# Splitting the first stage's result on two engines instead of one: ScalarE copies, GpSimd subtracts

## The reference

```python
Q = (X @ Wq.T + bq).reshape(B, S, H, d_head) * scale      # B=2, S=256, D=256, H=16
K = (X @ Wk.T + bk).reshape(B, S, H, d_head) * scale
V = (X @ Wv.T + bv).reshape(B, S, H, d_head)
scores = jnp.where(causal, einsum('bqhd,bkhd->bhqk', Q, K), -inf)
out = softmax(scores) @ V          # then @ Wo.T + bo
x = _layernorm(x + out)            # one [16, 128, 256] tensor
```

## Time and profile before

| | |
|---|---|
| median of three runs | 1124.04 us |
| the profiled execution | 1125.8 us, with a span of 1123.7 us |
| mean granted TensorE clock | 0.94 |
| TensorE busy | 994.0 us (88%) |
| VectorE busy | 885.0 us (79%) |
| ScalarE busy | 638.4 us (57%) |
| GpSimd busy | 538.6 us (48%) |
| DMA, mean | 95 GB/s |

### The profile page before, as it was taken

One profiled execution on the slowest core, in us unless ns is written; L12 is line 12 of the kernel. 1 busy time (PEld: TensorE's weight loads), 2 busy tenths in 40 slices (PEclk: granted clock), 3 DMA queues, 4 the chain that ended last, 5 costly groups with the idle time before them and its releaser, 6 DMA issues. The chain is left out here.

```text
span 1123.7 us, 25370 instructions
## 1 busy us (share of the span) xinstructions
PE 994.0 (88%) x8610; PEld 735.7 (65%) x8610; DVE 885.0 (79%) x2031; ACT 638.4 (57%) x1626; POOL 538.6 (48%) x983
## 2 busy tenths in 40 slices
PE   4769889973998977899999999999996999979996
PEld 3547666641565635788888888888884666546664
DVE  1458898932897966899999999999756899758885
ACT  2334555521798952555555555555443999944553
POOL 6347677873355643244444444444433465533322
PEclk8889999976899986899999999999998999989999
DMA  7989999843678530001001011111300566411111
GB/s 138 180 206 184 206 194 177 165 81 102 161 186 189 142 104 15 11 29 39 29 29 30 29 34 30 36 32 54 90 20 29 160 170 170 115 34 44 57 57 33
DMA packets 131550, 106.46 MB, mean 95 GB/s; under 512 B 16176, under 2 KB 124000, under 8 KB 131424
## 3 DMA queue, kind: packets, MB, share of 16 engines
q1 hardware_dynamic: 117952, 93.72, 35.6%
q10 hardware_dynamic: 11504, 8.98, 2.9%
q0 software_dynamic: 1968, 2.16, 1.2%
HBM read 64.97 MB, written 29.43 MB: 84 GB/s over the span
## 5 line engine op out<-in xcount | busy, mean ns | idle before, releaser
L406 DVE TENSOR_REDUCE ca_nm<-p_p 128x2 f32<-128x512 f32 x256 | 162.8, 677 | 16.0 <-PE p_p L304 14.3
L543 ACT ACTIVATE ca_pt<-p_p 128x512 f32<-128x512 f32 x256 | 142.6, 598 | 12.2 <-PE p_p L323 7.0
L304 PE MATMUL p_p<-ca_ks,ca_qs 96*128 96x256 bf16 x512 | 102.5, 285 | 18.1 <-DMA ca_ks<-k_stack 16.7
L1916 ACT ACTIVATE la_pq<-p_p,la_nm 128x128 f32<-128x128 f32 x256 | 90.3, 366 | 38.0 <-DVE la_nm L2019 38.0
L323 PE MATMUL p_p<-ca_qs,ca_ks 128*128 128x256 bf16 x512 | 101.3, 281 | 6.1 <-ACT ca_qs L535 2.4
L62 POOL TENSOR_TENSOR ca_pt<-la_lt,one 64x1024 f32<-64x1024 f32 x32 | 60.5, 1889 | 61.7 <-ACT la_lt L1895 60.5
L535 ACT ACTIVATE ca_qs<-p_p 32x1024 bf16<-32x1024 bf16 x64 | 65.1, 1017 | 40.4 <-PE p_p L313 38.9
L1900 ACT ACTIVATE la_qq<-p_p 128x512 f32<-128x512 f32 x32 | 19.1, 598 | 99.1 <-PE p_p L1732 99.1
L1070 DVE TENSOR_REDUCE sa_nm<-sa_p_s 128x4 f32<-128x512 f32 x64 | 43.6, 685 | 37.7 <-PE sa_p_s L930 37.3
L304 PEld LDWEIGHTS p_p<-ca_ks,ca_qs 96*128 96x128 bf16 x512 | 50.9, 102 | 31.5 <-DMA ca_ks<-k_stack 17.7
L1763 PE MATMUL p_p<-ca_pt,la_qq 128*128 128x128 f32 x512 | 70.9, 282 | 0.3 <-POOL ca_pt L62 0.3
(11 more groups left out here) (265 smaller groups left out, 2763.6 us busy)
## 6 DMA issues: line engine op xcount, KB each, us to landing
sa_qks<-sa_qkp SPq DMA_DIRECT2D x96, 128.0 KB, 5.3
ca_qs<-q_stack SPq DMA_DIRECT2D x32, 384.0 KB, 4.4
ca_ks<-k_stack SPq DMA_DIRECT2D x32, 384.0 KB, 5.3
ca_ct<-in_ctx_t SPq DMA_DIRECT2D x32, 128.0 KB, 5.1
ca_xr<-x_state SPq DMA_DIRECT2D x32, 128.0 KB, 2.1
x_state<-ca_xn SPq DMA_DIRECT2D x32, 128.0 KB, 2.1
k_stack<-sa_cxp SPq DMA_DIRECT2D x16, 192.0 KB, 2.8
q_stack<-sa_parts SPq DMA_DIRECT2D x16, 192.0 KB, 2.8
```

Of the source, the lines that this page charges most:

```text
L304: last = pe.matmul(p_s[n % 3][:, qc, :], QS[b % 4][0:STACK, h, 128 * qc:128 * qc + 128], KS[b % 4][0:STACK, h, :], start=True, stop=True)
L406: dve.tensor_reduce(NM[b % 2][:, h, :], p_s[n % 3][:, :, :], AX.X, ALU.max, negate=True).then_inc(max_done, 1)
L543: act.activation(PT[g][:, j, :, :], p_e[n % 2][:, :, :], ACT.Exp, scale=SCALE).then_inc(exp_done, 1)
L1916: last = act.activation(PQ[g % 2][:, j, :], p_s[g % 2][:, j, :], ACT.Exp, bias=NM[b % 2][:, 4 * g + j:4 * g + j + 1], accum_out=SM[g % 2][ ...
```

## The change

The result's split is taken off GpSimd in part. Its two copies (L62 on `sa_parts`) become ScalarE activations with `ACT.Copy`: `split_high(b - 2)` in slot 1 of step b, behind the exponentials and the high part of the context, and `split_middle(b - 2)` in slot 3, right behind the exponentials and ahead of the middle part of the context and the bias. The two subtractions stay on GpSimd but no longer stand together: `split_rest(b - 2)` is where the whole split was, `split_low(b - 2)` comes after `rstd(b - 1)` and `add_bias(b)`. The one counter `split_steps` becomes four semaphores; SyncE's stack stores wait for the last of them, `x_lo`. At the end of the stage the pairs follow each other in the same order.

```diff
@@ sync: store(b)
-                sp.wait_ge(split_steps, 4 * b + 4)
+                sp.wait_ge(x_lo, b + 1)
@@ gpsimd
-            def split(b):
-                pool.wait_ge(xn_done, b + 1)
-                wait(pool, xn_stored[b % 2], 16 * STORES * (b // 2))
-                wait(pool, split_steps, 4 * b)
-                split3(pool, XN[b % 2][:, :], parts[b % 2], rest[:, :], split_steps, 4 * b,
-                       lambda to, x: pool_copy(pool, sh, to, x))
+            def split_rest(b):
+                pool.wait_ge(x_hi, b + 1)
+                wait(pool, x_mid, b)
+                wait(pool, x_lo, b)
+                pool.tensor_tensor(rest[:, :], XN[b % 2][:, :], parts[b % 2][:, 0], ALU.subtract).then_inc(x_rest, 1)
+
+            def split_low(b):
+                pool.wait_ge(x_mid, b + 1)
+                pool.tensor_tensor(parts[b % 2][:, 2], rest[:, :], parts[b % 2][:, 1], ALU.subtract).then_inc(x_lo, 1)
@@ gpsimd: step(b)
                 if b >= 2:
-                    split(b - 2)
+                    split_rest(b - 2)
                 if later(b):
                     max_parts(b + 1, 1)
                 if b:
                     rstd(b - 1)
                     add_bias(b)
+                if b >= 2:
+                    split_low(b - 2)
                 if front(b):
                     query_key_rest(b + 3)
@@ gpsimd: after step 13, and at the end
                     pool.wait_ge(xb_done, b + 1)
+                    pool.wait_ge(x_lo, b - 1)
                     set_picks(pool, sh, picks_set)
-            split(B - 2)
+            split_rest(B - 2)
+            split_low(B - 2)
             rstd(B - 1)
-            split(B - 1)
+            split_rest(B - 1)
+            split_low(B - 1)
@@ scalar
+            def split_high(b):
+                act.wait_ge(xn_done, b + 1)
+                wait(act, xn_stored[b % 2], 16 * STORES * (b // 2))
+                act.activation(parts[b % 2][:, 0, :], XN[b % 2][:, :], ACT.Copy).then_inc(x_hi, 1)
+
+            def split_middle(b):
+                act.wait_ge(x_rest, b + 1)
+                act.activation(parts[b % 2][:, 1, :], rest[:, :], ACT.Copy).then_inc(x_mid, 1)
@@ scalar: step(b), after context_high in slot 1
+                    if g == 1 and b >= 2:
+                        split_high(b - 2)
+                    if g == 3 and b >= 2:
+                        split_middle(b - 2)
@@ scalar: at the end
             copy_out(B - 1)
+            split_high(B - 2)
+            split_middle(B - 2)
             copy_heads(B - 1)
+            split_high(B - 1)
+            split_middle(B - 1)
```

More of the change, by code:

```diff
@@ L741, in self_attention @@
         xn_done = sem("xn_done")
-        split_steps = sem("split_steps")
+        x_hi, x_rest, x_mid, x_lo = sem("x_hi"), sem("x_rest"), sem("x_mid"), sem("x_lo")
         xn_stored = [sem(f"xn_stored{u}") for u in range(2)]
```

## The result

The changed kernel takes 1134.68 us (median of five runs, 1132.82 to 1137.15) against 1124.04 us; the ratio is 1.0088 with a 95% interval of 1.0063 to 1.0112. Six more runs of it beside 29 of the kernel before, in a later comparison, gave 1.0098 (1.0067 to 1.0129). The forecast was 1128.6 us, slower, in a range up to 1135.5: the direction and the mechanism are right, the size is half of what came. Executions of one kernel spread by up to 13 us here (the kernel before: 1117.42 to 1130.7 in 29 runs), so a single trace shows where time goes, and the ratios say how much. A ratio takes in all runs of both kernels; it need not be the quotient of the two medians.

A forecast was written before the change was run, and what follows sets the result against it. GpSimd was taken to sit in the first stage's loop, with stack loads on SyncE having 0.7 us of slack or none. Terms +3.8 + 2.0 - 1.5 + 0.7 - 0.4 = +4.6 us gave 1128.6 us, range 1121.5 to 1135.5.

The forecast's parts named there:

- The late stores: On SyncE, stack stores wait for the later lower part, so the last stack load is issued at A + 7.6 us.
- A: The end of `add_bias` on GpSimd in a step, from which SyncE's stores and loads are timed.
- The three late steps: Steps 10 to 12 of the first stage: 13.53 us each instead of 12.27, +3.8 us in all.
- K: Time from A to the first scores two steps on: 13.6 us, against 10.5 before.
- third rival: Slower than forecast: TensorE waits lower the clock (2 us) and loads land slowly; +10.7 us, 1134.7 us, chance 0.15.
- the loop over two steps: First scores to A, then A to the scores two steps on: (13.45 + 13.6) / 2 = 13.5 us a step.
- The seven earlier steps: Steps before the three late ones, averaging 14.07 us: most of the delay hides there, +2.0 us (bounds 0 and 5).
- Step 13: Step without weight quantization: TensorE waits less for GpSimd's maxima, -1.5 us (bounds -1.9 and 0).
- `picks` and the end: After step 13 `split_low` precedes `picks`, +0.7 us; at the stage's end copies are faster on ScalarE, -0.4 us.
- The relief: Copies leaving GpSimd free the port shared with VectorE: L1430 took 1.04 us beside a copy, 0.69 without.
- My first rival: Faster: engines bound the steps, not the stores; -4.7 us, 1119.3 us, chance 0.15.
- ScalarE: Two copies of 0.41 us each added there: high one free, middle one ahead of the bias 0 (bounds 0 and 0.4).

The follow-up runs named there:

- Experiment 1: Changed kernel with SyncE issuing the late stack stores behind the next step's stack loads: 1118.12 us, ratio 0.9977; repeated, 1120.57 us, ratio 0.9966.
- 4: Changed kernel with the last subtraction of the split ahead of `rstd` and `add_bias` instead of behind them: 1126.89 us, ratio 1.0019.
- experiment 5: Changed kernel with GpSimd's scale of the quantized weights behind `split_rest` instead of ahead of the maxima: 1135.74 us, ratio 1.0101.
- experiments 2: Kernel before the change, with SyncE's stack loads put ahead of the late stores: 1125.55 us, ratio 1.0003.
- 8: Changed kernel with the loads first, plus two GpSimd copies into tiles nobody reads: 1125.30 us, ratio 1.0010.
- both orders: Stack loads ahead of the late stores and the scale behind the split: kernel before 1120.68 us, ratio 0.9973; changed kernel 1118.75 us, ratio 0.9956.
- experiment 7: Changed kernel with ScalarE's middle copy behind the bias instead of ahead of it: 1135.34 us, ratio 1.0092.

## Why the prediction was right in kind and short in size

**The late stores.** Right, step by step: the `q_stack` issues behind L1178 and L1195, the residual's load at A + 3.8, the last stack load starting at A + 7.6 in step 10 (208.5, with A = 200.95) and landing 6.3 us later, where 6.0 was taken. In step 11 it started only at A + 8.7, one issue before it having taken 1.76 us, and landed after 4.8: the same sum. Experiment 1 takes it away and 4 shortens it; both do what this chain says.

**The three late steps: the term that was mis-sized.** Forecast 13.53 us a step, +3.8 in all; measured 14.65, +7.1. K is not the reason: by its own loads it was 13.6 to 13.9. The step that failed is X, from the first scores to A, held at 13.45 in all three. It was 14.1 us in step 10, 16.9 in step 11 (200.24 to 217.17) and 13.9 in step 12, and the 3.5 us of step 11 make up the missing 3.3. In step 11 VectorE's lock made TensorE wait for 1.99 us, and the clock of 0.57 over the 4 us behind it cost about another 1.7 (an estimate: 4 x 0.43). The forecast had put the clock at nothing; only the third rival priced it, at 2 us.

How much of this is the change and how much one execution, a second profile of the changed kernel shows, from the run beside the repeat of experiment 1 (steps 10, 11 and 12):

```profile
190.01:204.80 14.79, 11.71 (x131) 8.54 (x129) 11.47 (x27) 8.90 (x22) 11.35 (x20) 1.00 0.80 143
204.80:217.24 12.44, 11.73 (x128) 8.58 (x129) 11.13 (x25) 6.77 (x17) 5.32 (x14) 1.00 0.95 170
217.24:231.71 14.47, 12.38 (x128) 8.61 (x129) 11.99 (x28) 8.59 (x22) 11.02 (x20) 1.00 0.64 130
```

Here the clock stayed at 1.00, X was 13.3, 13.7 and 13.6 us, and the steps took 41.70 us, 13.9 each: +4.9, near the forecast of +3.8. Where the clock holds, the loop over two steps comes out. In experiment 5 the lock was nearly gone and the three steps still averaged 14.6; there too X of step 11 was long, 15.8 us, at half clock behind the wait for the loads. What decides whether the clock falls is open: it fell behind 2.86 us there and stayed at 1.00 behind 2.84 us in this second profile.

**The seven earlier steps.** Forecast +2.0, measured +3.9 at step 10, of which 1.4 was there at step 3, so +2.5 in these steps; +3.7 in the second profile. I had also taken the second scores of step 3 (84.47) for its first (83.31); their average is 14.2 us, not 14.07, which changes nothing in the argument.

**Step 13.** Forecast -1.5 with -1.9 as its end; measured -3.4. TensorE's wait of 1.86 us for the maxima is gone. It seems to have had a price in clock too, which came back with it: the granted clock of the step went from 0.80 to 0.87, worth about 1.6 us (an estimate: 16.78 x 0.20 less 13.36 x 0.13).

**`picks` and the end.** Forecast +0.3, measured +0.9 from step 14 on.

The sum of the measured terms, +3.9 + 7.1 - 3.4 + 0.9, is the 8.5 us of the profiled executions. The medians lie 10.6 us apart, and two profiles can't say where the other 2 us are. One slip in the range: X - 0.4 and a landing of 5 give 12.8 us a step, not 12.9, which moves its lower end by 0.2 us.

**The relief.** VectorE's L1430 took 0.69 us on average in steps 3 to 12 after, against 0.90 before, where the row showed 1.04 and 0.69. The Trainium skill's rule on the shared ports ("SBUF — State Buffer", "Who interferes with whom") holds here for VectorE by L1443 and L1430, and for GpSimd by its L62 at 221.83, 0.65 us instead of 0.20 while VectorE's L1449 ran until 222.42. By itself it would have had the change faster, and with the stores out of the way the medians and ratios lie that way: 1.0003 against 0.9977 in experiments 2 and 1, back at 1.0010 in 8, and 0.9973 against 0.9956 with both orders. My first rival was this case, 4.7 us faster; what the runs show of it is 0.2% to 0.3%, 2 to 3 us, not clear of noise, and it was covered by 14 us of late stores.

**The third rival**, a lower clock with slow landing at 1134.7 us, has the number that came, and half of its reason. Its lower clock was there, in step 11 of the profiled execution; its slow landing was not, at most 6.3 us in steps 10 and 11. That the median came within 0.1 us of it is luck.

**ScalarE.** Costed at 0, and experiment 7 finds none.

## What to carry to other kernels

When a step of a chain is split over engines and a part of it moves to a later place in the order, look up who waits for its end, and what stands behind that wait on the waiting queue: here a store nobody needed soon held six loads that the next scores needed. Put loads with a near deadline ahead of stores that wait for late data. When a change adds waits of 1 to 3 us on TensorE, give the granted clock a term of its own: here the same kernel's three late steps took 43.94 us in one profile and 41.70 in another, and the first had the half clock in it.

## What the runs showed of the hardware beyond that

VectorE instructions on 128x16 elements took 0.17 us alone and up to 1.15 us beside a GpSimd instruction of 1.16 us; L1103 on 128x256 went from 0.40 to 1.36. The loss is about 1 us in both, so the smallest instructions lose the most for their length. TensorE's clock was at 0.57 in the mean from 208 to 212 us, behind a wait of 1.99 us, and stayed at 1.00 behind one of 1.28 us at the start of step 10, in a kernel that is busy on TensorE for 84% of those steps. In other executions it was at 0.50 for 5 us behind a wait of 2.86 us and at 1.00 behind one of 2.84 us: the length of the wait alone does not tell.
